# A two-layer delta-rule tower on one core: the second layer's products on four quarters of the array, values scaled by key lengths after the solve

## The chip, the cores and the metric

The kernel runs on one core of a Trainium2 chip. The metric is the device time of one execution in microseconds (us). One core has TensorE (PE in the profile, with its weight loads as PEld), VectorE (DVE), ScalarE (ACT), GpSimd (POOL) and SyncE (SP). Each takes its own instructions in order, and they wait for each other through semaphores.

## The reference, cut to what matters

The tower turns 16 images of 49 tokens (width 256) through two layers. Both have an attention that is a recurrence over tokens; the first layer has 4 heads, the second 16, each with 64 key and 64 value elements. The second layer's:

```python
q = q / (jnp.linalg.norm(q, axis=-1, keepdims=True) + EPS)
k = k / (jnp.linalg.norm(k, axis=-1, keepdims=True) + EPS)
alpha = jax.nn.sigmoid(h @ alpha_w + alpha_b).reshape(bsz, seq, H, DK)
beta = jax.nn.sigmoid(h @ beta_w + beta_b)
def step(s, inp):
    qt, kt, vt, at, bt = inp
    s = s * at[..., None]
    u = jnp.einsum('bhd,bhdv->bhv', kt, s)
    s = s + bt[..., None, None] * (kt[..., None] * (vt - u)[..., None, :])
    out = jnp.einsum('bhdv,bhd->bhv', s, qt)
    return (s, out)
...
y = y * jax.lax.rsqrt(jnp.mean(y * y, axis=-1, keepdims=True) + EPS) * head_norm_w
y = x + y @ out_w * gate
```

The first layer's has no decay `alpha`. Only the 16x49 outputs of the whole tower are returned, not the state.

## The kernel before, in words

The recurrence is not stepped through. For each image and head the kernel builds a 49x49 matrix A of key-key products and PT of key-query products, inverts a triangular system, and applies the result. An image pair lies on the 128 partitions: the even image's tokens on partitions 0 to 48, the odd one's on 64 to 112. All arithmetic on TensorE is f32; there each product of two f32 operands stands in the trace as two weight loads and two matmuls, a transpose as one of each.

The stages in order of time, with the time of the profile: patches and projections (0 to 65), the first layer's pairs, solve and applied products (65 to 122), layernorms and routing, the expert stage (181 to 280), the second layer's "level" stage (322 to 470: `small`, L1517, 32 products of 64x49 each in 56 calls on the four quarters of the array, with projections L1477 between), its solve (470 to 508), its applied products (510 to 575), the output projection (575 to 601), and two feed-forward parts.

Class `Delta` holds solve and application for both layers; the first uses its subclass `WideDelta`. For each layer:

- `dve_lengths` makes inverse key lengths (`inv_k`), `beta_k`, `beta_kk`. `pe_cols` and `pe_rows` turn beta and the rows of A into the layout of the solve (systems on partitions). In the second layer `pe_rows` is 48 transposes of 128x128, in 12 groups of 4 (L420); DVE multiplies each group by beta into `NS` (L459).
- `dve_solve`: 24 steps of two DVE instructions each (L473 and L479; in the first layer L809 and L815), each on what the last wrote.
- `pe_out` and `act_out` turn the solved rows back, on PE and ACT, during the solve; the second layer's value projections (L1528) fill PE there. `act_mask` scales A by a column (L519).
- `pe_apply`: for head h four products of 49x49 by 49x64, each for 8 image pairs and both partition halves, 16 matmuls: `d1` = U W (L570), `z` = A d1 (L580), `delta` = U W again after W was corrected (L591), `out` = PT delta (L602). Iteration i does d1 of head i, z of i-1, delta of i-3, out of i-5, so there are nh+5 iterations. Both inputs and output of a matmul lie on one partition half, so consecutive matmuls alternate between two diagonal quarters of the array. Each kind of product has two PSUM banks, used in turn by even and odd heads.
- Between them: ACT copies d1 (L655); DVE multiplies z by `inv_k` (L702) and POOL subtracts that from W (L394); ACT and DVE copy delta and out in turn; then squares, sums, root, reciprocal and a scaling by DVE (L731) make the normalised y, which PE turns (L554) and projects (L612).

What sets the order is this hand-written order of each engine's stream and the waits in it; nothing is scheduled by a program.

## Time and profile before

| | us |
|---|---|
| runs of before | 713.9, 717.19, 720.05 |
| their median | 717.19 |
| the profiled execution | 716.03 |
| its span, first to last instruction | 714.2 |
| PE busy in the span | 631.0 (88%) |
| granted TensorE clock, mean | 0.945 of full speed |

The profile is of one execution. In it 1.8 us lie outside the span. The page gives busy time by engine; the timeline gives instructions in order of time, and in square brackets the idle time of the engine before one and what ended it. "issue" there means that the engine waited for no semaphore that the profile shows. The DMA queue called "instruction" carries the engines' own programs from memory.

### The profile page before, as it was taken

The numbers are of one execution on the slowest core, as the hardware profiler recorded it, in microseconds if no ns is written. First come the engines' busy times: TensorE is split into PE (matmuls) and PEld (weight loads), VectorE is DVE, ScalarE is ACT, GpSimd is POOL, SyncE is SP. The second block draws the span as 40 slices with busy tenths as digits, with TensorE's granted clock in tenths as the row PEclk, the third lists the DMA queues.
The fourth block names the chain that finished last, engine by engine and source line by source line (L and its number), as shares of the span: only waits on it lengthen the run. The fifth ranks groups of instructions, "written<-read, shape, count | busy, mean of one in ns | idle before, by whom it ended". The sixth has DMA issues, their size and how long they took to land.

```text
span 714.2 us, 20162 instructions
## 1 busy us (share of the span) xinstructions
PE 631.0 (88%) x9124; PEld 463.7 (65%) x9124; DVE 329.0 (46%) x519; ACT 268.6 (38%) x538; POOL 144.4 (20%) x129
## 2 busy tenths in 40 slices
PE   8985497973899996699999997999899999999997
PEld 5654495673799995465655556665699966555563
DVE  0395735730011110356777779569536753411311
ACT  0354233211233232244666664548634443111223
POOL 9101030012000001712544446400133200000000
PEclk9997579996999999699999999799999999999999
DMA  9200000018989871100000201000000070000001
GB/s 315 110 0 2 4 3 2 1 36 313 409 316 335 324 268 33 49 15 31 26 27 26 84 4 62 3 3 0 2 5 4 5 295 1 1 0 0 1 1 45
DMA packets 20229, 56.38 MB, mean 79 GB/s; under 512 B 4272, under 2 KB 13104, under 8 KB 15792
## 3 DMA queue, kind: packets, MB, share of 16 engines
q1 hardware_dynamic: 19376, 53.00, 20.2%
q0 software_dynamic: 768, 2.10, 0.9%
q8 instruction: 72, 1.18, 0.7%
q14 instruction: 13, 0.11, 0.0%
HBM read 49.57 MB, written 5.52 MB: 77 GB/s over the span
## 4 chain that ended last, share of the span: by engine, by line
PE 73%; DVE 14%; issue 4%; ACT 3%; DMA 2%; POOL 2%; SPq 1%; DVEq 0%; ACTq 0%; POOLq 0%
PE PS L1477 8%; PE PS L1439 6%; PE PS L1517 6%; PE PS L1428 6%; PE PS L1614 6%; PE PS L612 4%; PE PS L1644 3%; PE PS L1621 3%; PE PS L570 3%; PE PS L591 3%; PE PS L580 3%; PE PS L602 3%; PE PS L1320 2%; PE PS L1334 2%; DVE arena L1773 2%
## 5 line engine op out<-in xcount | busy, mean ns | idle before, releaser
L1517 PEld LDWEIGHTS PS<-arena 64*49 64x49 f32 x3584 | 50.6, 124 | 37.2 <-issue 21.9
L1477 PE MATMUL PS<-Y,arena 128*128 128x392 f32 x192 | 73.3, 511 | 0.0
L1517 PE MATMUL PS<-arena 64*49 64x48 f32 (+2 forms) x3584 | 57.0, 214 | 11.1 <-DVE arena L1773 6.6
L1428 PE MATMUL PS<-arena 128*128 128x128 f32 x448 | 54.1, 280 | 4.8 <-DMA arena<-in_moe_b 4.2
L1768 DVE COPY_PREDICATED arena<-msk,PS 128x768 f32<-128x768 int32 x24 | 44.9, 1873 | 28.5 <-PE PS L1517 28.5
L1428 PEld LDWEIGHTS PS<-arena 128*128 128x128 f32 x448 | 53.5, 196 | 6.4 <-DMA arena<-in_moe_b 4.8
L1192 ACT ACTIVATE arena<-PS,arena 128x128 f32<-128x128 f32 x112 | 31.8, 369 | 65.2 <-PE PS L1428 65.2
L1130 POOL TENSOR_TENSOR arena<-arena 128x384 f32<-128x384 f32 (+1 forms) x32 | 36.1, 1128 | 78.5 <-PE PS L1517 73.9
L1439 PE MATMUL PS<-arena 128*128 128x256 f32 x224 | 50.5, 379 | 0.0
L394 POOL TENSOR_TENSOR arena<-arena,work 128x512 f32<-128x512 f32 x20 | 25.4, 1270 | 114.0 <-DVE work L702 114.0
L1477 PEld LDWEIGHTS PS<-Y,arena 128*128 128x128 f32 x192 | 33.2, 188 | 19.2
L1439 PEld LDWEIGHTS PS<-arena 128*128 128x128 f32 x224 | 41.5, 190 | 5.1
L1614 PE MATMUL PS<-work,arena 128*128 128x392 f32 x128 | 43.4, 491 | 0.8 <-issue 0.8
L1717 DVE COPY arena<-PS 128x256 f32<-128x256 f32 x14 | 5.9, 425 | 65.8 <-PE PS L1418 65.8
L1614 PEld LDWEIGHTS PS<-work,arena 128*128 128x128 f32 x128 | 24.0, 188 | 18.9 <-issue 1.1
L219 PE MATMUL PS<-fill 128*128 128x256 bf16 x236 | 31.5, 286 | 2.1 <-DVE fill L1667 2.1
L1103 POOL DMA_INDIRECT arena<-answers,place x8 | 7.6, 951 | 118.0 <-DMA answers<-arena 115.9
L1843 DVE TENSOR_TENSOR arena<-arena,PS 128x392 f32<-128x392 f32 x16 | 9.0, 563 | 47.2 <-ACT arena L1294 47.2
L702 DVE TENSOR_TENSOR work<-PS,inv_k 128x512 f32<-128x512 f32 x20 | 13.8, 690 | 34.6 <-PE PS L580 34.6
L219 PEld LDWEIGHTS PS<-fill 128*128 128x128 bf16 x236 | 23.6, 103 | 9.2 <-DVE fill L1667 2.1
L1528 PE MATMUL PS<-work,Y 128*128 128x512 f32 x64 | 29.0, 595 | 0.0
L612 PE MATMUL PS<-arena 128*128 128x392 f32 x80 | 27.7, 493 | 1.3 <-issue 1.3
(230 smaller groups left out, 1141.0 us busy)
## 6 DMA issues: line engine op xcount, KB each, us to landing
arena<-in_moe_w SPq DMA_DIRECT2D x28, 1024.0 KB, 6.3
arena<-in_qka_w SPq DMA_DIRECT2D x8, 384.0 KB, 3.1
arena<-in_patches SPq DMA_DIRECT2D x6, 392.0 KB, 6.6
arena<-in_ff_w SPq DMA_DIRECT2D x1, 2048.0 KB, 8.3
arena<-in_ffn_w SPq DMA_DIRECT2D x2, 1024.0 KB, 12.7
by_expert<-arena SPq DMA_DIRECT2D x1, 1792.0 KB, 12.7
arena<-in_moe_b SPq DMA_DIRECT2D x14, 128.0 KB, 7.4
arena<-by_expert SPq DMA_DIRECT2D x14, 128.0 KB, 6.9
```

Source lines behind the costliest of these rows:

```text
L219: nc.tensor.matmul(PS[:, i, 0:2 * P], fill[:, 0:P], fill, start=True, stop=True)
L394: nc.gpsimd.tensor_tensor(w, w, self.ZT[h % 2], ALU.subtract).then_inc(self.s["w_kept"], 1)
L612: m = nc.tensor.matmul(bank(4 + u), self.OW[:, f, (u // 2) * P:(u // 2 + 1) * P], half(self.OT[:, f], u % 2), start=(f == 0), stop=(f == n ...
L1130: nc.gpsimd.tensor_tensor(older, older, end, ALU.mult).then_inc(lv_keys, 1)
L1192: nc.scalar.activation(G[:, j % 2, f], PS[:, 4 + 2 * (j % 2) + f // 4, (f % 4) * P:(f % 4 + 1) * P], ACT.Gelu, bias=MB1[j % NW][:, f:f + 1 ...
L1428: m = nc.tensor.matmul(PS[:, 4 + 2 * (j % 2) + f // 4, (f % 4) * P:(f % 4 + 1) * P], MW1[j % NW][:, k, f * P:(f + 1) * P], XT[:, j % 2, k] ...
L1439: m = nc.tensor.matmul(PS[:, 2 + j % 2, 0:D], G[:, j % 2, f], MW2[j % NW][:, f], start=(f == 0), stop=(f == FT - 1))
L1477: m = nc.tensor.matmul(bank(i % 3), GW[g % 2][:, k, u // 2], half(Y[:, k], u % 2), start=(k == 0), stop=(k == KT - 1))
L1517: m = nc.tensor.matmul(o, K[r, b, :], v, start=True, stop=True)
L1528: m = nc.tensor.matmul(PS[:, value_bank(u), :], Y[:, k, 2 * b:2 * b + 2].rearrange("p b t -> p (b t)"), VW[:, k, n * 512:(n + 1) * 512], s ...
L1614: m = nc.tensor.matmul(bank(4 + 2 * n + cc), FW13[:, k, cc, f * P:(f + 1) * P], half(SQ[:, k], n), start=(k == 0), stop=(k == KT - 1))
L1768: nc.vector.copy_predicated(dst, mk, src).then_inc(lv_kept, 1)
```

## The change

It does the following:

1. The values are scaled once, before the products: POOL multiplies each head's W by the key lengths kept in `root`. In the second layer POOL waits for the last solve step, in the first only for the lengths. W is then corrected by a single DVE subtraction out of PSUM; POOL's subtraction, `inv_k`'s masking and `beta_k` go. Correspondingly the first 25 token columns of A are cleared and only the rest masked (`act_mask` and `act_clear`).
2. In the second layer (`PARTS` 2) a product's input half and output half are chosen apart: for a pair of images the four matmuls go to quarters (0,0), (0,1), (1,0), (1,1). The result of odd images lands on the other partition half, so A and PT of every second image pair are built swapped already in `small`. A product now uses both banks of its kind, so head h waits until head h-1 is copied away (`ahead` 1, before 2). The number of matmuls is unchanged.
3. The second layer's `pe_rows` is no longer 48 full transposes but 192 ordinary matmuls of 64 partitions by 49 columns on the four quarters, in 6 groups of 32; DVE takes 6 products twice as large.
4. The second layer's final scaling of y moves from DVE to POOL; squares, sums and roots stand one iteration later in both layers.
5. The first layer (`PARTS` 1) keeps its two banks in turn and its order of matmuls.

```diff
-            NGI = (T - 1) // 4
+            NGI = (T - 1) // 8
-            def pool_apply(self, pool):
-
+            def pool_apply(self, pool, values_kept):
+
+                pool.wait_ge(*values_kept)
+                if self.PARTS == 2:
+                    self.wait(pool, "step", 2 * (BL - 1))
+                else:
+                    self.wait(pool, "lengths", self.n_lengths)
                 for h in range(self.nh):
-                    self.wait(pool, "z_kept", h + 1)
                     w = self.W[:, :, h * DH:(h + 1) * DH]
-                    nc.gpsimd.tensor_tensor(w, w, self.ZT[h % 2], ALU.subtract).then_inc(self.s["w_kept"], 1)
+                    key = root[:, self.S + h * BP:self.S + (h + 1) * BP].unsqueeze(2).broadcast_to([P, BP, DH])
+                    nc.gpsimd.tensor_tensor(w, w, key, ALU.mult).then_inc(self.s["w_scaled"], 1)
+                if self.PARTS == 2:
+                    for j in range(self.nh // 2):
+                        self.scale(pool, nc.gpsimd, j)
...
-                for r in range(4):
-                    m = nc.tensor.transpose(PS[0:self.S, g % 4, r * P:(r + 1) * P],
-                                            self.Am[:, :, 1 + 4 * g + r], c("ident"))
+                for r in range(8):
+                    for place_ in range(2):
+                        for odd in range(2):
+                            p = slice(TP * place_, TP * place_ + TP)
+                            m = nc.tensor.matmul(
+                                PS[TP * odd:TP * odd + TP, 2 * (g % 2) + (place_ + odd) % 2, r * TP:r * TP + T],
+                                self.Am[p, odd::2, 1 + 8 * g + r], c("ident")[p, TP * place_:TP * place_ + T],
+                                start=True, stop=True)
...
+            def product(self, i, h, operands):
+
+                for pair in range(0, BP, 2):
+                    for r, o in ((0, 0), (0, 1), (1, 0), (1, 1)):
+                        b = (r + o) % 2
+                        if self.PARTS == 1:
+                            r, b, o = o, r, o
+                        lhsT, rhs = operands(self.part(r), pair + b)
+                        m = nc.tensor.matmul(self.place(i, h, self.part(o), pair + b), lhsT, rhs, start=True, stop=True)
+                return m
...
+                        self.wait(pe, "w_scaled", h + 1)
+                        if h >= self.ahead:
+                            self.wait(pe, "d1_kept", h + 1 - self.ahead)
...
-                        nc.vector.tensor_tensor(
-                            self.ZT[h % 2], PS[:, 2 + h % 2, :].rearrange("p (b v) -> p b v", b=BP),
-                            inv_k[:, h * BP:(h + 1) * BP].unsqueeze(2).broadcast_to([P, BP, DH]),
-                            ALU.mult).then_inc(self.s["z_kept"], 1)
+                        nc.vector.tensor_tensor(self.head(h), self.head(h), self.result(1, h), ALU.subtract) \
+                            .then_inc(self.s["w_kept"], 1)
...
-                            o = PS[TP * (b % 2):TP * (b % 2) + T, pb + hd]
+                            c_ = (b + pair) % 2
+                            o = PS[TP * c_:TP * c_ + T, pb + hd]
```

The order of PE's instructions at the start of the second layer's solve, before; L1517 are the last level products, L420 the rows of A turned by transposes, L1528 value projections:

```order
L1517 MATMUL PS<-arena 49x64 x32
L411 MATMUL PS<-con,beta_kk 128x128
L412 MATMUL PS<-con,beta_k 128x128
L1528 MATMUL PS<-work,Y 128x512 x2
L1517 MATMUL PS<-arena 49x64 x32
L420 MATMUL PS<-con,arena 128x128 x48
L1528 MATMUL PS<-work,Y 128x512 x6
L502 MATMUL PS<-con,arena 128x128 x8
```

The same place after the change; L1566 is L1517 of before, L438 the rows of A, L1577 the value projections:

```order
L1566 MATMUL PS<-arena 49x64 x32
L426 MATMUL PS<-con,beta_kk 64x128 x2
L1577 MATMUL PS<-work,Y 128x512 x2
L1566 MATMUL PS<-arena 49x64 x32
L438 MATMUL PS<-con,arena 64x49 x192
L1577 MATMUL PS<-work,Y 128x512 x6
L521 MATMUL PS<-con,arena 128x128 x8
```

Nothing moved there, but 48 instructions became 192, and these are ordinary f32 products, which count twice in the trace.

POOL's last instructions, before; L394 is the subtraction from W:

```order
L387 MEMSET arena 128x3400
L387 MEMSET arena 128x2x25
L1130 TENSOR_TENSOR arena<-arena 128x16x6x4
L1133 TENSOR_TENSOR arena<-arena 128x16x6
L1130 TENSOR_TENSOR arena<-arena 128x16x2x8
L1133 TENSOR_TENSOR arena<-arena 128x16x3
L1121 TENSOR_TENSOR arena<-arena 128x16
L394 TENSOR_TENSOR arena<-arena,work 128x8x64 x16
```

And after the change; L398 scales W by the key lengths, L407 is the final scaling of y that DVE had:

```order
L386 MEMSET arena 128x3400
L386 MEMSET arena 128x2x25
L1175 TENSOR_TENSOR arena<-arena 128x16x6x4
L1178 TENSOR_TENSOR arena<-arena 128x16x6
L1175 TENSOR_TENSOR arena<-arena 128x16x2x8
L1178 TENSOR_TENSOR arena<-arena 128x16x3
L1166 TENSOR_TENSOR arena<-arena 128x16
L398 TENSOR_TENSOR arena<-arena,root 128x8x64 x16
L407 TENSOR_TENSOR arena<-arena,y_var 128x8x128 x8
```

The sixteen instructions on W keep their place in POOL's stream but no longer wait for each head's z, and eight on y come behind them.

## Rows read from the trace of the kernel before

**Rows 1.** The page, parts 1 (busy us, share, instructions) and 3 (packets, MB, share).

```profile
PE 631.0 (88%) x9124; PEld 463.7 (65%) x9124; DVE 329.0 (46%) x519; ACT 268.6 (38%) x538; POOL 144.4 (20%) x129
q8 instruction: 72, 1.18, 0.7%
```

**Rows 2.** Busy time of each engine in three stretches.

```profile
core 0: us, PE busy (x) PEld busy (x) DVE busy (x) ACT busy (x) POOL busy (x), PEclk, DMA share, GB/s
76.60:92.40 15.80, 6.91 (x196) 6.00 (x196) 13.09 (x48) 4.46 (x15) 0.00 (x0) 0.50 0.01 3
470.30:477.40 7.10, 6.94 (x58) 6.27 (x52) 4.50 (x14) 2.07 (x2) 0.00 (x0) 1.00 0.02 3
509.90:574.80 64.90, 62.03 (x2064) 60.06 (x2065) 36.62 (x55) 30.03 (x53) 20.28 (x16) 1.00 0.04 7
```

**Rows 3.** Timeline of weight loads, second layer's products: start, us, engine, line, idle before.

```profile
537.88 0.17 PEld L580 LDWEIGHTS PS<-arena 49*49 49x49 f32 x3 [0.27 <-issue]
...
540.64 0.88 PEld L580 LDWEIGHTS PS<-arena 49*49 49x49 f32 x28
541.81 0.17 PEld L580 LDWEIGHTS PS<-arena 49*49 49x49 f32 x4 [0.29 <-issue]
...
556.34 1.01 PEld L580 LDWEIGHTS PS<-arena 49*49 49x49 f32 x32
557.24 1.01 PEld L591 LDWEIGHTS PS<-arena 49*49 49x49 f32 x32
```

**Rows 4.** DMA of 532 to 544 us: GB/s in 40 slices, the instruction queue.

```profile
GB/s 0 0 0 0 0 0 0 0 0 0 55 0 0 0 0 0 0 0 0 0 0 0 0 55 0 0 0 0 0 0 0 0 0 0 0 0 55 0 0 0
...
q8 instruction: 3, 0.05, 2.0%
```

**Rows 5.** DMA of 554 to 564 us, the same two rows.

```profile
GB/s 0 0 66 0 0 0 0 0 0 0 0 0 0 0 0 0 66 0 0 0 0 0 0 0 0 0 0 0 0 0 0 66 0 0 0 0 0 0 0 0
...
q8 instruction: 3, 0.05, 1.9%
```

**Rows 6.** DMA of 466 to 482 us, GB/s in 40 slices of 0.4 us.

```profile
GB/s 0 0 0 0 0 0 0 0 0 0 41 0 0 0 20 0 0 0 0 0 0 0 0 0 0 0 0 0 0 0 0 0 0 20 0 0 0 41 0 0
```

**Rows 7.** Timeline of PE in the level stage, products on four quarters.

```profile
348.51 1.12 PE L1517 MATMUL PS<-arena 64*49 64x64 f32 x64
349.56 1.58 PE L1477 MATMUL PS<-Y,arena 128*128 128x392 f32 x4
...
354.36 1.68 PE L1517 MATMUL PS<-arena 64*49 64x49 f32 x128
355.97 1.25 PE L1477 MATMUL PS<-Y,arena 128*128 128x392 f32 x3
```

**Rows 8.** Timeline at the start of the second layer's solve.

```profile
472.63 4.06 PE L420 MATMUL PS<-con,arena 128*128 128x128 f32 x32 [0.16 <-ACT arena L1237]
473.41 3.68 DVE L459 TENSOR_TENSOR arena<-PS,sys_cols 128x192 f32<-128x192 f32 x8 [0.54 <-PE PS L420]
477.36 0.35 DVE L473 TENSOR_TENSOR work<-arena 128x96 f32<-128x96 f32 x1
```

**Rows 9.** Timeline where DVE and POOL both read two operands from SBUF.

```profile
339.26 1.77 DVE L1773 TENSOR_TENSOR arena<-arena 128x1568 f32<-128x1568 f32 x1
339.57 2.01 POOL L1130 TENSOR_TENSOR arena<-arena 128x256 f32<-128x256 f32 x1 [2.77 <-PE PS L1517]
340.96 1.67 DVE L1796 TENSOR_TENSOR arena<-arena 128x384 f32<-128x384 f32 x2
```

**Rows 10.** Instructions of POOL's line L394: duration min, median, max in ns.

```profile
L394 POOL TENSOR_TENSOR arena<-arena,work x20: 1263/1270/1276, 98.1 to 564.7; 128x512 f32<-128x512 f32 x20
```

**Rows 11.** Timeline of the first layer: lengths, start of the solve, first products.

```profile
73.03 0.19 DVE L436 TENSOR_TENSOR beta_kk<-beta_k,inv_k 128x32 f32<-128x32 f32 x1
...
76.58 0.20 DVE L809 TENSOR_TENSOR work<-arena 128x24 f32<-128x24 f32 x1 [0.52 <-DVE arena L801]
...
92.47 3.65 PE L570 MATMUL PS<-arena 49*49 49x64 f32 x64 [0.69 <-issue]
```

More of the change, by code:

```diff
@@ L378, in wait @@
                 eng.wait_ge(self.s[name], self.before.get(name, 0) + value)
-            NGI = (T - 1) // 4
+            NGI = (T - 1) // 8
             NGO = len(GROUPS)
-            ZT = [work[:, 1024 + 512 * i:1536 + 512 * i].rearrange("p (b v) -> p b v", b=BP) for i in range(2)]
             def pool_clear(self, pool):
@@ L542, in kept, with place, result, ahead @@
                     self.wait(eng, f"{what}_{('even', 'odd')[h % 2]}", h // 2 + 1)
+            def product(self, i, h, operands):
[7 more added lines that the diff above has]
+                return m
+            def place(self, i, h, part, b):
+                if self.PARTS == 2:
+                    return PS[part, 2 * i + b % 2, (b // 2) * DH:(b // 2 + 1) * DH]
+                return PS[part, 2 * i + h % 2, b * DH:(b + 1) * DH]
+            def result(self, i, h):
+                if self.PARTS == 2:
+                    return PS[:, 2 * i:2 * i + 2, 0:BP // 2 * DH].rearrange("p a (m v) -> p a m v", v=DH)
+                return self.pairs(PS[:, 2 * i + h % 2, :].rearrange("p (b v) -> p b v", b=BP))
+            @property
+            def ahead(self):
+                return 3 - self.PARTS
+            def pairs(self, x):
+                return x.rearrange("p (m a) v -> p a m v", a=2)
+            def head(self, h):
+                return self.pairs(self.W[:, :, h * DH:(h + 1) * DH])
             def pe_apply(self, pe, between=None):
@@ L586, in pe_apply @@
                         self.wait(pe, "w_kept", h + 1)
-                        self.kept(pe, "delta", h - 2)
-                        for b in range(BP):
-                            for cc in range(2):
-                                r = self.part(cc)
-                                m = nc.tensor.matmul(PS[r, 4 + h % 2, b * DH:(b + 1) * DH],
-                                                     self.U[r, h, b, :], self.W[r, b, h * DH:(h + 1) * DH],
-                                                     start=True, stop=True)
-                        m.then_inc(self.s["delta_mm"], 1)
+                        self.kept(pe, "delta", h - self.ahead)
+                        self.product(2, h, lambda r, b: (self.U[r, h, b, :], self.W[r, b, h * DH:(h + 1) * DH])) \
+                            .then_inc(self.s["delta_mm"], 1)
                     h = i - 5
@@ L597, in pe_apply @@
                         self.kept(pe, "delta", h)
-                        self.kept(pe, "out", h - 2)
-                        for b in range(BP):
-                            for cc in range(2):
-                                r = self.part(cc)
-                                m = nc.tensor.matmul(PS[r, 6 + h % 2, b * DH:(b + 1) * DH],
-                                                     self.PT[r, h, b, :], self.D[r, h, b, :], start=True, stop=True)
-                        m.then_inc(self.s["out_mm"], 1)
+                        self.kept(pe, "out", h - self.ahead)
+                        self.product(3, h, lambda r, b: (self.PT[r, h, b, :], self.D[r, h, b, :])) \
+                            .then_inc(self.s["out_mm"], 1)
                     if 0 <= i - self.nh - 1 < self.EARLY:
@@ L640, in keep_out @@
                 self.wait(eng, "out_mm", h + 1)
-                op(self.W[:, :, h * DH:(h + 1) * DH],
-                   PS[:, 6 + h % 2, :].rearrange("p (b v) -> p b v", b=BP)).then_inc(self.s[f"out_{('even', 'odd')[h % 2]}"], 1)
+                op(self.head(h), self.result(3, h)).then_inc(self.s[f"out_{('even', 'odd')[h % 2]}"], 1)
             def keep_delta(self, eng, op, h):
                 self.wait(eng, "delta_mm", h + 1)
-                op(self.D[:, h], PS[:, 4 + h % 2, :].rearrange("p (b v) -> p b v", b=BP)) \
+                op(self.pairs(self.D[:, h]), self.result(2, h)) \
                     .then_inc(self.s[f"delta_{('even', 'odd')[h % 2]}"], 1)
             def act_apply(self, act, between=None):
-                for i in range(self.nh + 8):
+                for i in range(self.nh + 9):
                     if between is not None:
@@ L694, in dve_apply @@
             def dve_apply(self, dve):
-                for i in range(1, self.nh + 9):
+                for i in range(1, self.nh + 10):
                     h = i - 1
```

131 lines of the change are left out of this document (67 added, 64 removed).

## The prediction

> **What bounds the kernel now.** The page comes first: PE is busy 88% of the span, so the path runs mostly through PE [rows 1]. The windows by stage come next, for the stages that the change touches. In the second layer's applied products PE shows 62 of 64.9 us busy, DVE 37, ACT 30, POOL 20 [rows 2]. Read alone, this says that PE's arithmetic is the bound and that twice the quarters should nearly halve the stage. In the first layer's solve DVE is busy 13.1 of 15.8 us [rows 2], a chain of dependent steps.
>
> The timeline of the weight loads says something else about the applied products. A product is 16 matmuls, so 32 loads and 32 matmuls in the trace, and undisturbed ones follow each other every 0.90 us (556.34 to 557.24). But at 537.88 and at 541.81 PE stops in the middle of a product for "issue", which is no semaphore, and goes on with the last 3 or 4 loads [rows 3]. From one restart to the next are 3.93 us where four products take 3.6. The loads between the restarts are 3 + 32 + 32 + 32 + 28 = 127 (three rows of 32 are left out), with as many matmuls and a few waits: 256 instructions.
>
> The page has 9124 loads and as many matmuls, with about 250 waits 18,500 instructions, and 72 transfers on the instruction queue, of 1.18 MB / 72 = 16.4 KB [rows 1]: again one per 256 instructions. The DMA view places them. In 532 to 544 us, slices of 0.3 us, they begin in slices 10, 23 and 36, that is at about 535.1, 539.0 and 542.9, 3.9 us apart; 2.0% of 16 engines over 12 us is 3.84 us, 1.28 us each [rows 4]. So the transfer begun at 535.1 ends at 536.4, PE restarts 1.45 us later at 537.88, and the next transfer begins 1.2 us after that. I read this as a loop: entering a block of 256 instructions asks for the next, whose transfer starts 1.2 us later, and it can be used 1.4 us after its end. One round is 2.6 us plus the transfer. At 554 to 564 us a transfer took 1.9% x 160 / 3 = 1.01 us, they begin 3.5 to 3.75 us apart [rows 5], the loop needs 3.6, four products need 3.6, and no stall stands there [rows 3]. The stage is therefore already at the edge of two limits, arithmetic (3.6 us per iteration) and the supply of instructions (3.6 to 3.9, on the average of the stage's transfers, 1.1 us, 3.7).
>
> The Trainium skill (Runtime: NRT & Kernel Launch, Instruction fetch mechanics) says that instructions are refilled in 16 KiB blocks of 256, which the trace agrees with, and that PE's store holds 2048 of them and crossing a block's edge is "mostly hidden". The stalls of 0.27 and 0.29 us [rows 3] speak against the second half. By the page the sum would be that of rival 1, by the row that of the forecast.
>
> **The change part by part.** *Applied products, second layer.* Their number stays 64, with 64 instructions each, 4096. Four-quarter products are in the trace: 64 loads of 49 columns with 64 columns streamed take 349.56 - 348.51 = 1.05 us, and 128 with 49 streamed take 1.61 us [rows 7]. A new product, 32 loads, is then 0.40 to 0.53 us of PE; I take 0.50, near the row with 64 columns, but its operand is contiguous. Arithmetic needs 4 x 0.50 = 2.0 us per iteration, DVE and ACT somewhat above 2, the instruction supply still 3.7. So the supply sets the pace. With the waits the stage is about 4190 instructions. Counted in blocks of 256 back from the restart at 541.81 and then forward through the changed stream, an edge stands some 175 instructions into the stage; the blocks up to there and one beyond are at hand, and PE enters the second about 1.9 us in, held by the chain d1, copy, d1. Fifteen more edges come at 3.7 us: 57.4 us. The last 170 instructions, the last copy of out and the two turns take 3.9 as they do now. That is 61.3 against 64.9: **-3.6 us** (transfers of 1.0 us: -5; of 1.2 us: -2). What has only one set of banks now (head h waits for the copy of h-1) costs nothing here: each product has 0.93 us on average while a copy takes 0.6 to 0.7. That cover goes if the supply is not the limit.
>
> POOL's scaling of W starts when the solve ends. One is 1.27 us like L394 [rows 10], about what `pe_out` and `act_out` need behind the last step anyway, and the next heads come every 1.25 us, faster than they are used. Sixteen take 20 us. The scalings of y have twice the elements, 2.5 us each, eight in a stage where two heads take 7.4 us, and the last must be ready only when the projection reaches it, seven periods of 3.5 us later. Both 0, as is the moved DVE work.
>
> *`pe_rows`, second layer.* Before: 48 transposes, 96 instructions, from 470.3 with the last 32 at 472.63 for 4.06 us, then the first solve step at 477.36 [rows 8]. Behind stands the whole solve, in which DVE never rests, so a delay here moves everything. New: 192 matmuls, 768 instructions, three blocks. Arithmetic alone would be 6 x 0.81 us (32 matmuls of 49 columns [rows 7]), a little less than now. The supply: by the same count an edge stands 114 instructions before the first one, so the next stand at 149, 405 and 661. A transfer begins in slice 10 of 0.4 us, at 470.4 [rows 6], and the block is usable at 470.4 + 1.1 + 1.4 = 472.9. The edges are then passed at 472.9, 476.6 and 480.3 (3.7 each), and the remaining 107 instructions take 0.7: 481.0. The last DVE multiply (twice 192 elements; 0.36 us for 192 at most, from L459 [rows 8]; 0.6 taken) and the diagonal: first step at 482.0, **+4.6 us**. Bounds 3.7 to 5.5, by transfers of 0.8 to 1.4 us. If no block is late it is -0.6.
>
> *First layer.* The lengths are done near 73.2 [rows 11], and POOL then runs four scalings of 1.25 us, to 78.3. The solve begins at 76.58, and each of its instructions reads two operands in SBUF. Such instructions exclude POOL's: at 339.57 a POOL multiply of 256 elements starts under a DVE one and shows 2.01 us, until 341.58, and the two DVE instructions issued at 340.96 show 1.67, so they end 1.05 us after 341.58 [rows 9]; nobody ran until the other had ended. So the first step waits for the third scaling (about 77.0), the second for the fourth (78.5): +1.9 us in a chain that PE waits for. Four small matmuls and a DVE step less give 0.2 back. **+1.7 us** (0, if DVE always wins, to 2.5). Its products keep order and pitch: 0. The Trainium skill (SBUF — State Buffer, Who interferes with whom) tells of the same lock and lets the first to issue keep it.
>
> *Level stage.* Where odd image pairs come in swapped order, a quarter is used again after 3 matmuls instead of 4. With 48 or 49 columns that is still enough; with 64, 3 x 33 = 99 ns lie under the 107 that one needs (128 cycles at 2.4 GHz, twice). Bounds 0 and 16 calls x 0.05 us = 0.8; **+0.3 us**.
>
> Sum: -3.6 + 4.6 + 1.7 + 0.3 = **+3.0 us**. The profiled execution took 716.0, 1.2 under the median. So 719.0 against it, 720.2 against the median; I forecast 720. Its own range is 715 to 725.
>
> **The rivals.** *1. Instructions are at hand, arithmetic bounds.* For it speak PE's busy share and that the stalls before are only 0.3 us; against it the equal distance of transfer, restart and transfer in rows 3 to 5. Then the stage is bounded by DVE, about 35 us of work with the scalings of y gone [rows 2], and PE 64 x 0.50 = 32, with some 7 us to fill and drain: 42, so -23. `pe_rows` gives -0.6, the other two +2.0: -21.6, about 695. Chance 0.12, with cases halfway (two blocks ahead).
>
> *2. The clock falls, the other side.* PE now works 2.0 us of each 3.7 in the stage. In the first layer's solve, with PE 6.9 of 15.8 us busy, the granted clock is 0.50 [rows 2], 1.2 of 2.4 GHz, and two products then take 3.65 us instead of 1.8 [rows 11]. At half clock a four-quarter product is 1.0 to 1.06 us and an iteration 4.0 to 4.25, above the supply's 3.7. It decides from 3.7 / 4 = 0.93 us per product, a clock under 0.57. Over 15 iterations up to +8 us: 728. Against it: the second layer's solve keeps its clock. Chance 0.08.
>
> *3. The supply bounds, but `pe_rows` is spared,* since a block more was ready there in the calm before. Then +3.0 - 4.6 = -1.6, 715.5. The first part of the stage before was short of nothing at 470 [rows 8], but 768 instructions are more than any two blocks. Chance 0.12.
>
> **How the numbers follow.** Forecast 0.68, rivals 0.12, 0.08 and 0.12. About 1% of this kernel, 7 us, can be told from no change. Forecast and rival 3 lie within it, but for the forecast's upper end (first layer 2.5, rows 5.5, products 0: +9) with 0.07. Faster by over 1%: 0.12; slower: 0.15; within: 0.73. The range 712 to 727 leaves out rival 1 and the far end of rival 2.
>
> **What the profile after would show.** Transfers on the instruction queue in the applied products still 3.5 to 3.9 us apart, PE idle for "issue" about 1.7 us per iteration, products of 0.5 us; 75 transfers in all; the first solve step of the second layer 4 to 5 us later behind the last level product, with PE stopped for "issue" twice or three times inside L438; the first layer's L809 and L815 with one or two instructions of over 1 us. I am wrong if transfers come 2.5 us apart, if the products' stage is under 50 us, or if the granted clock falls in it.

## The result, and the profile after

The changed kernel is slower: 730.9 us median of four runs (728.3 to 740.2) against 718.6 (713.9 to 720.1), a ratio of 1.0191 with a 95% interval of 1.0135 to 1.0247. The execution of 740.2, with a mean granted clock of 0.87 against 0.90 to 0.92 in the others, counts as a slow one and is left out of the ratio. In a later session it was 728.9 against 717.5, ratio 1.0158 (1.0111 to 1.0204). The forecast was 720, the range 712 to 727. The profiled execution took 728.33 us, its span is 726.0 (before 716.03 and 714.2), so the two traces differ by 11.8 us of span.

The page after, parts 1 and 3 (compare [rows 1]), and busy time by stage (compare [rows 2]; the first stretch is the first layer's solve, then `pe_rows`, then the second layer's products):

```profile
PE 621.7 (86%) x9454; PEld 451.9 (62%) x9454; DVE 320.0 (44%) x503; ACT 269.8 (37%) x540; POOL 154.6 (21%) x137
q8 instruction: 75, 1.23, 0.7%
```

```profile
core 0: us, PE busy (x) PEld busy (x) DVE busy (x) ACT busy (x) POOL busy (x), PEclk, DMA share, GB/s
76.50:93.60 17.10, 6.90 (x197) 6.03 (x197) 14.29 (x48) 4.47 (x15) 2.31 (x5) 0.50 0.01 3
476.60:489.90 13.30, 12.91 (x405) 12.31 (x394) 3.51 (x7) 2.06 (x2) 0.00 (x0) 0.87 0.02 6
522.60:586.60 64.00, 40.37 (x2064) 36.63 (x2065) 30.16 (x49) 30.08 (x52) 24.00 (x20) 0.92 0.02 4
```

In the products PE is busy 40.4 us instead of 62.0, and the stage is only 0.9 us shorter (64.0 for 64.9). `pe_rows` and what stands between it and the first solve step takes 13.3 us instead of 7.1. Timeline of the weight loads in the products (compare [rows 3]):

```profile
535.99 1.85 PEld L585 LDWEIGHTS PS<-arena 49*49 49x49 f32 x126 [1.44 <-issue]
539.94 5.34 PEld L585 LDWEIGHTS PS<-arena 49*49 49x49 f32 x252 [2.10 <-issue]
546.81 1.85 PEld L585 LDWEIGHTS PS<-arena 49*49 49x49 f32 x126 [1.53 <-issue]
550.81 1.85 PEld L585 LDWEIGHTS PS<-arena 49*49 49x49 f32 x126 [2.15 <-issue]
554.82 1.85 PEld L585 LDWEIGHTS PS<-arena 49*49 49x49 f32 x126 [2.17 <-issue]
558.32 1.80 PEld L585 LDWEIGHTS PS<-arena 49*49 49x49 f32 x124 [1.65 <-issue]
```

126 loads with their matmuls and waits are one block of 256 instructions. They are done in 1.85 us, and then PE stands for "issue" until the next block is there, 3.5 to 4.0 us after the last one. That is the pattern that the forecast described. Timeline of `pe_rows` and the first solve step after (compare [rows 8]):

```profile
476.63 2.45 PEld L438 LDWEIGHTS PS<-con,arena 64*64 64x64 f32 x75
479.60 9.35 PEld L438 LDWEIGHTS PS<-con,arena 64*64 64x64 f32 x309 [0.52 <-issue]
...
489.94 0.33 DVE L492 TENSOR_TENSOR work<-arena 128x96 f32<-128x96 f32 x1
```

Only the first of the three block edges stops PE. After it 309 loads run without a pause and take 9.35 us, 30 ns each. In the first layer (timelines of POOL and DVE; compare [rows 10, 11]):

```profile
73.33 4.05 POOL L398 TENSOR_TENSOR arena<-arena,root 128x512 f32<-128x512 f32 x4 [9.78 <-DVE beta_kk L455]
...
75.64 0.78 DVE L846 COPY arena<-sys_cols 128x25 f32<-128x25 f32 x1
76.53 0.89 DVE L854 TENSOR_TENSOR work<-arena 128x24 f32<-128x24 f32 x1
77.45 0.35 DVE L860 TENSOR_TENSOR arena<-arena,work 128x24 f32<-128x24 f32 x1
77.83 0.33 DVE L854 TENSOR_TENSOR work<-arena 128x46 f32<-128x46 f32 x1
...
77.34 1.47 POOL L1136 TENSOR_TENSOR arena<-con,par 128x128 f32<-128x128 f32 x4
```

A copy that took 0.18 us and a first step's first instruction that took 0.20 take 0.78 and 0.89 under POOL's scalings. The copy costs nothing, since the solve begins as long behind the rows as before (5.0 us). A scaling takes 1.04 us, not 1.27, so they end at 77.4 and hold up one instruction of the solve for long. Behind them run four short multiplications of POOL (L1136), which before stood beside the first layer's products. Under them four instructions of the solve take 0.33 to 0.35 us instead of 0.21 to 0.23. Of the 1.2 us by which the first product comes late, 0.7 are that first instruction and 0.5 these four.

The shift between the two traces, read at the start of the same instructions, gives the sum by stage (us, rounded; `pe_rows` runs from its first load to the first solve step):

| stretch | forecast | measured |
|---|---|---|
| rows to first product, first layer | +1.7 | +1.2 |
| first product to the experts' end, same code but for order | 0 | +3.3 (1.0, 0.6, 2.4, then -0.7) |
| gather and norm to the first level product | 0 | +1.2 |
| level stage but its last call | +0.3 | -0.3 |
| last level call, same work | 0 | +1.0 |
| `pe_rows` | +4.6 | +6.3 |
| second solve | 0 | 0.0 |
| applied products | -3.6 | -0.8 |
| sum, before rounding | +3.0 | +11.8 |

### The profile page after: what moved, and what is told of

Read it like the earlier page. It is cut to its first block and busy times, and to the rows that moved or that the text cites. A ratio compares the mean times of both kernels' runs of the same rounds, so it can differ in the third digit from the quotient of the medians.

```text
span 726.0 us, 20823 instructions
## 1 busy us (share of the span) xinstructions
PE 621.7 (86%) x9454; PEld 451.9 (62%) x9454; DVE 320.0 (44%) x503; ACT 269.8 (37%) x540; POOL 154.6 (21%) x137
## 5 line engine op out<-in xcount | busy, mean ns | idle before, releaser
L585 PE MATMUL PS<-arena 49*49 49x64 f32 x2560 | 55.4, 230 | 23.7 <-issue 20.8
L1566 PEld LDWEIGHTS PS<-arena 64*49 64x49 f32 x3584 | 50.9, 125 | 36.8 <-issue 21.4
L585 PEld LDWEIGHTS PS<-arena 49*49 49x49 f32 x2560 | 51.7, 131 | 27.9 <-issue 25.2
L1566 PE MATMUL PS<-arena 64*49 64x48 f32 (+2 forms) x3584 | 57.2, 215 | 10.7 <-DVE arena L1822 6.7
L1766 DVE COPY arena<-PS 128x256 f32<-128x256 f32 x14 | 5.9, 425 | 65.5 <-PE PS L1466 65.5
L398 POOL TENSOR_TENSOR arena<-arena,root 128x512 f32<-128x512 f32 x20 | 20.1, 1044 | 56.8 <-DVE arena L498 47.0
L1577 PE MATMUL PS<-work,Y 128*128 128x512 f32 x64 | 29.2, 599 | 0.0
```

Of the source, the lines that this page charges most:

```text
L585: m = nc.tensor.matmul(self.place(i, h, self.part(o), pair + b), lhsT, rhs, start=True, stop=True)
L1566: m = nc.tensor.matmul(o, K[r, b, :], v, start=True, stop=True)
L1577: m = nc.tensor.matmul(PS[:, value_bank(u), :], Y[:, k, 2 * b:2 * b + 2].rearrange("p b t -> p (b t)"), VW[:, k, n * 512:(n + 1) * 512], s ...
```

## The experiments

**1. Is the supply of instructions the pace of the products?** Two kernels from the changed one.

```
# half_products                                   # more_instr, ahead of each matmul of layer 2
-for pair in range(0, BP, 2):                     +nc.tensor.matmul(self.place(...)[:, 0:1], lhsT, rhs[:, 0:1],
+for pair in range(0, BP, 2 * self.PARTS):        +                 start=True, stop=True)
```

> The changed kernel, with every second pair of matmuls of the second layer's applied products left out (32 instructions a product instead of 64; 2048 in the stage instead of 4096). The output is not the reference's. Copies on ACT and DVE, scalings on POOL and the waits are all unchanged. Changed kernel: 64.0 us from the first L585 load to the first load of the projection, restarts 3.7 us apart. Supply theory: 7 to 8 block edges instead of 15; the supply alone would need 28 us, so the chain through ACT and DVE sets the pace and the stage takes 40 to 46 us, with blocks taken less often than every 3.7 us and few or no stops at their edges. Rival (the single set of banks, that is the chain product, copy, next product, sets the pace and the stops are only its shadow): nothing of that chain but 0.25 us per product has gone, and the stage stays at 58 us or more.

> The changed kernel, with a matmul of one column ahead of each matmul of the second layer's applied products, into the same place and overwritten by it: 128 instructions a product instead of 64, 8192 in the stage, the same result. PE stands idle 1.4 to 2.0 us of each 3.7 in the changed kernel, and the added loads and matmuls need at 12 to 16 ns a pair about 1.5 to 2 us of it. Supply theory: an iteration is two blocks and takes 2 x 3.7 = 7.4 us, the stage 15 more edges x 3.7 = +55 us, the whole kernel about 780 to 788. Rival (arithmetic, or the chain of copies, bounds and the supply does not): the additions fit into PE's idle time, the stage takes 64 to 75 us.

Measured, from the first load of the products to the first of the projection: 40.6 us with half the instructions, 120.5 us with twice as many (+56.5 for +55 forecast), and the whole kernels took 710.5 and 782.9 us, one execution each. Both numbers are those of the supply theory. But the granted clock fell in both. The stage in half_products, in more_instr and in after_fill (the changed kernel with other work ahead of it, experiment 3):

```profile
526.50:567.10 40.60, 34.79 (x1042) 31.13 (x1041) 28.92 (x49) 29.21 (x52) 23.99 (x20) 0.58 0.01 3
519.20:639.70 120.50, 107.49 (x4112) 100.16 (x4112) 30.77 (x50) 31.13 (x53) 24.36 (x20) 0.54 0.02 4
514.20:579.00 64.80, 52.98 (x2065) 49.27 (x2065) 30.29 (x49) 30.59 (x52) 24.36 (x20) 0.68 0.02 4
```

In more_instr PE is busy 107.5 of 120.5 us at a mean clock of 0.54, so PE's own work is nearly as long as the supply's: this run alone doesn't tell them apart. What speaks for the supply there are stops of 0.4 to 1.1 us for "issue" at most block edges. In half_products transfers come 4.5 us apart on average, so the supply is no longer the pace there; whether the 40.6 us are the chain of copies or PE at the lower clock is not separated. The cleaner evidence is the third row. Over nine profiles of the stage in quarters with 4096 instructions PE is busy between 40.4 and 53.0 us, at mean clocks from 0.92 down to 0.68, and the stage takes 62.8 to 67.2 us without following it: 64.0 at 40.4, 64.8 at 53.0. PE's arithmetic is not the pace. DMA of 540 to 556 us in more_instr, slices of 0.4 us:

```profile
GB/s 0 0 0 41 0 0 0 0 0 0 0 0 41 0 0 0 0 0 0 0 0 41 0 0 0 0 0 0 0 0 41 0 0 0 0 0 0 0 41 0
q8 instruction: 5, 0.08, 2.1%
```

Transfers begin every 3.5 us here, and every 3.7 on average of the stage. Over the fifteen profiles of the products with 4096 instructions, on the diagonal or in quarters, the mean distance is 3.7 to 3.9 us and the mean transfer 1.03 to 1.12.

**2. Why do `pe_rows`' loads take 30 ns?** rows_probe changes the stationary operand from group to group, rows_swap the count of matmuls.

```
# rows_probe: groups 3, 4          lhsT = self.W[p, 0, TP * (2 * r + odd):TP * (2 * r + odd) + TP]
# rows_probe: groups 5, 6          lhsT = self.Am[p, odd:odd + 2 * T - 1:2, 1 + 8 * g + r]
# rows_swap: 96 matmuls over all 128 rows; for odd systems x is the identity with halves exchanged
+x = bass.AP(x.tensor, x.offset + TP, [x.ap[0], [-TP, 2], [1, TP]])
+m = nc.tensor.matmul(o, self.Am[:, odd::2, 1 + 8 * g + r], x, start=True, stop=True)
```

> The changed kernel, with other operands in the second layer's pe_rows: groups 1 and 2 as they are (64 stationary columns, read 196 bytes x 2 apart), groups 3 and 4 with 64 stationary columns that lie side by side (taken from W), groups 5 and 6 with 49 columns at the old distance. The output is not the reference's, since four of six groups turn other numbers. In the changed kernel L438 issues its 384 loads in 12.0 us, about 30 ns each, with one stop of 0.5 us only, where the prediction had 12.6 ns each and stops at two more block edges. Theory A (the distance between the columns makes a load long, so that quarters don't overlap): groups 3 and 4 take 0.8 to 1.0 us each without the stops, groups 5 and 6 about 1.5 (49/64 of 2.0), and PE stops for issue once or twice in or behind groups 3 and 4, since 256 instructions then need less than the supply's 3.7 us. Theory B (the width or the form of the tile, 64 columns for 49): groups 3 and 4 stay at 2.0 us, groups 5 and 6 fall to 0.8. Theory C (the supply of instructions paces it smoothly): all six groups stay near 1.9 us.

The timeline of L443's loads in rows_probe: the four stretches begin behind the stops at block edges.

```profile
471.73 2.45 PEld L443 LDWEIGHTS PS<-con,arena 64*64 64x64 f32 x75
474.70 2.83 PEld L443 LDWEIGHTS PS<-con,arena 64*64 64x64 f32 x128 [0.52 <-issue]
478.17 2.62 PEld L443 LDWEIGHTS PS<-con,arena 64*64 64x64 f32 x128 [0.63 <-issue]
481.89 1.36 PEld L443 LDWEIGHTS PS<-con,arena 64*49 64x49 f32 x53 [1.10 <-issue]
```

(The distance is 784 bytes, two systems of 98 elements, not 2 x 196 as my expectation had it.) By start-to-start distances without the stops, a load took 29.5 ns in groups 1 and 2, 15 ns in groups 3 and 4 (side by side) and 22.7 in groups 5 and 6 (49 columns at a distance). Theory A holds, theories B and C fall: where loads are short, the three stops that the forecast expected are there (0.5, 0.6, 1.1 us); where they are long, PE is the slower one and no further stop is seen behind the first.

> The changed kernel, with pe_rows by 96 matmuls over all 128 rows instead of 192 over 64: one matmul turns 64 systems of one token, and for odd systems the identity is read with its halves exchanged. So 96 x 64 = 6144 stationary columns are loaded at a distance (twice, since f32 is loaded twice), against 12288 in the changed kernel and 6144 in 48 transposes before. Theory A (columns at a distance take 0.46 ns each per load, whatever the tile: rows_probe showed 29.5 ns for 64 of them, 22.7 for 49, and 15 ns for 64 side by side): L438 takes 5.7 us with a stop of about 0.6 us, 12.1 before it, and the kernel is 5.5 to 6.5 us faster than the changed one, 724 to 726 against its median of 730.9. Rival (the count of instructions bounds, 384 of them at 3.7 us per 256): the same 5.6 us, but with stops at the block edges; then the loads show under 25 ns. If pe_rows were not on the path, nothing changes.

Both answers fell, and so did the forecast of 724 to 726 us. L441 in rows_swap:

```profile
474.68 11.53 PEld L441 LDWEIGHTS PS<-con,arena 128*64 128x64 f32 x192
```

Half the loads, 59 ns each, the same 11.3 us start to start, and 729.7 us (ratio 1.0184, 1.0144 to 1.0225). So the price is not by column. For an operand at a distance it is by element: 64 x 64 elements take 29.5 ns, 128 x 64 take 59, and 128 x 128, the transposes before (392 bytes apart), 118 ns. What doubled is the number of loads per element: a matmul in f32 shows two loads, a transpose one (48 transposes are 48 loads in L420). 48 x 118 = 5.7 us before, 384 x 29.5 = 11.3 after, 192 x 59 = 11.3 here.

> both_swap with the even systems' rows turned by a transpose instead of a matmul with the identity (the odd ones stay matmuls with the exchanged identity). In rows_swap 192 loads of 64 columns took 11.3 us, 59 ns each, so the cost is not by column as I had thought but by element: 64 x 64 elements at a distance take 29.5 ns, 128 x 64 59 ns, 128 x 128 118 ns (48 transposes before, each with one load). A matmul in f32 loads its operand twice, a transpose once. Theory: the even half falls from 96 loads to 48, the rows take 144 x 59 ns = 8.5 us and the stop of 0.5, 2.8 us less than in both_swap. Rival (a transpose loads twice as well, or costs more per load): 11.3 us as in both_swap.

Measured: 744.0 us (1.0378). The transposes do show one load each and the matmuls two, but the 48 rows take 33 us, with the matmuls in L444 and the transposes in L446 (loads by line: count, busy us, mean ns, idle before):

```profile
L444 PEld LDWEIGHTS PS<-con,arena 128*64 128x64 f32 x96 | 14.9, 204 | 5.8
L446 PEld LDWEIGHTS PS<-con,arena 128*64 128x64 f32 x48 | 6.6, 137 | 5.8
```

That is 0.69 us per row instead of 0.24, far more than the 0.18 of its three loads: a transpose and a matmul in turn cost something of their own that this run doesn't split up. So the count of loads is seen, the gain from it could not be seen here. diagonal_l0 (experiment 4) shows it: it goes back to 48 transposes, in the 6 groups of the changed kernel but with the systems in the old order.

**3. What did the first layer cost?** l0_two takes half of POOL's scalings away from the solve; before_late puts the delay alone into the kernel before.

```
# l0_two, in pool_apply                       # before_late, ahead of the first step, five times
+if h == 2 and self.PARTS == 1:               +self.wait(dve, "unit", 1 + i)
+    self.wait(pool, "step", 2 * (BL - 1))    +nc.vector.tensor_copy(work[:, 0:P], c("ident")).then_inc(...)
```

> The changed kernel, with two of the first layer's four scalings of W on POOL moved behind the last step of its solve (the first two still run beside the lengths, from 73.3 to 75.4 us, the solve's first step comes at 76.5). Theory A (POOL's operations held up the solve): L854 and L860 show 0.2 us from the first step on, as in the kernel before, and the first product comes 1.1 us earlier behind the rows, 20.9 us instead of 22.0. Theory B for the clock (PE stays at 1.2 GHz longer only because of where the delayed solve puts the products): the first product to the first turn takes 21.4 instead of 22.4, the turn and projection 7.8 instead of 8.4, the routing 6.9 instead of 9.3; the kernel is 5 us faster, 726. Rival for the clock (it is the products' other order, or chance): only the 1.1 us come back, 729.8.

> The changed kernel once more, beside the same runs of before, for its median in the same session: 728 to 732 and a ratio near 1.018. l0_two measured 721.2 against it, 9.7 us less, of which 5 are explained (1.1 of solve, 4 at the lower clock). If the rest is chance of the runs, this median comes out lower, 726 to 728; if the scalings on POOL cost more than I know, it stays at 731.

base_after is the 728.9 us already given. l0_two: 721.2 us (1.0078, 1.0039 to 1.0116), more than the 5 us that I had expected. The medians differ by 7.7 us, but they come from two sessions; by the two ratios (1.0158 and 1.0078) it is 5.7. The first steps show 0.20 us again, and the first product comes 20.4 us behind the rows instead of 22.0. That is 1.6 us. From there to the end of the routing the profile is 4.1 us shorter, at the higher clock; what it gains behind that I leave to the scatter of single executions. Windows from the first product to the first turn, and of the routing that follows (PEclk is the column before the last two), in this order: before, the changed kernel, l0_two.

```profile
92.40:114.00 21.60, 16.65 (x513) 16.51 (x513) 9.60 (x15) 7.21 (x12) 6.51 (x8) 0.90 0.01 3
143.10:149.90 6.80, 6.80 (x52) 6.69 (x52) 1.59 (x7) 2.64 (x8) 0.00 (x0) 0.84 0.00 0
...
93.60:116.10 22.50, 17.64 (x512) 17.39 (x512) 9.54 (x15) 7.21 (x12) 0.00 (x0) 0.80 0.01 3
145.80:155.10 9.30, 9.21 (x52) 9.08 (x52) 1.59 (x7) 3.06 (x8) 0.00 (x0) 0.63 0.00 0
```

```profile
91.30:112.90 21.60, 16.64 (x513) 16.43 (x513) 9.60 (x15) 7.21 (x12) 2.46 (x6) 0.90 0.01 3
142.00:148.80 6.80, 6.79 (x52) 6.66 (x52) 1.59 (x7) 2.63 (x8) 0.00 (x0) 0.84 0.00 0
```

The granted clock has two levels, 0.50 and 1.00 (1.2 and 2.4 GHz), and the mean tells how long each stood. The same 52 matmuls take 6.8 us at a mean of 0.84 and 9.3 at 0.63; in the products 1.0 us is lost in the same way. I call 21.3 to 21.8 us with 6.8 or 6.9 behind it the short form, 22.2 to 22.6 with 9.3 the long one. All six profiles of kernels that carry the four early scalings (and no filling, below) have the long form. A second profile of the kernel before has the short one:

> The kernel before, once more, for a second profile of the stretches that the change doesn't touch. Between the two profiles the routing to the experts begins 1.6 us later than the first layer's end explains, the levels 1.2 us and the solve 1.3 us more: 4 us in stretches with the same code. Theory A (the time at half clock in these stretches varies from execution to execution, and has nothing to do with the change): this execution shows differences of 1 us or more to the first profile of before in the same stretches. Theory B (the later end of the first layer moves work so that PE's clock falls or recovers later): this execution repeats the first profile within 0.3 us in each stretch.

It took 21.3 and 6.9 us. In the stretches up to the levels it repeats the first profile within 0.3 us (theory B), but its second solve, at lower clock in between, took 2.7 us longer with the same code (theory A). Both are true in their place.

> The kernel before, with five dependent copies of 128 columns on DVE (about 0.23 us each) between the rows and the first step of the first layer's solve, so that this solve ends some 1.2 us later; nothing else is changed, the result is the same. Theory (a first product that comes 22.0 us behind the rows instead of 20.4 to 20.9 meets a lower clock for longer: in four executions of the changed kernel's kind TensorE rose to 2.4 GHz 5.6 to 6.3 us after the first product, in four with the early one 3.6 to 4.2 us after it, and the routing that follows took 9.3 instead of 6.8 us): the delay of 1.2 us costs 4 to 5.5 us, about 722 to 724, first product to first turn 22.3 to 22.6 us instead of 21.3 to 21.6, turn and projection 8.3 instead of 7.8, routing 9.3 instead of 6.9. Rival (the longer time at the lower clock comes from the changed kernel's order of products, or is chance): 1.2 us, 719.5.

Measured 720.3 (1.0042, 1.0009 to 1.0075), 2.9 over the 717.5 beside it. The profiled execution, one of its fastest, shows the delay (22.0 us) but the short form behind it, 21.8 and 6.8 us. Its twelve timings fall into two groups, three from 714.3 to 716.4 and nine from 719.1 to 722.7. The kernel before has such times too without the delay, but fewer (5 of 21 from 719.3 to 721.4 beside it). So the delay seems to make the long form frequent, not certain; that the nine are the long form is inferred from their times, not seen in a trace. both_swap (below) has the long form in its profile without the delay. When the granted clock changes is thus not bound to the kernel's steps: it rises 4.1 us after the first product in the kernel before and 4.5 in before_late, 6.3 in the changed kernel, and 4.2 in l0_two but 6.1 in both_swap, which have the same first layer. The Trainium skill (TensorE: Matmul & The Clock Gate, Part 1) says that the hardware's watch on activity doesn't start with the kernel; that the same code meets the rise at different places agrees with it.

The last question was whether the clock is all of it. Matmuls whose result nobody reads fill PE's waits of the first layer:

```
+spin(12, 6)                                       # ahead of pe_sums, and behind pe_cols
+spin((24, 14, 14, 14, 14, 6, 4, 0)[g], 6)         # ahead of each group of the first layer's pe_out
```

> The kernel before, with 114 matmuls of 256 bf16 columns whose result nobody reads, in PE's waits of the first layer: 12 ahead of pe_sums, 12 behind pe_cols, 24, 14, 14, 14, 14, 6 and 4 ahead of the groups of pe_out. At 2.4 GHz one takes 0.11 us, so they fit in the waits for DVE's solve; at 1.2 GHz they would not. Theory (activity on PE keeps the clock up, and the lower clock is what stretches this part): the granted clock stays at 1.00 from 63 us to the end of the first layer, the first product to the first turn takes 19.5 to 20 us instead of 21.3 to 21.6, the routing 6.9 or less; the kernel is 2 to 5 us faster, 713 to 716. Rival (the clock falls in spite of them): the added matmuls take twice as long, the groups of pe_out come late, 720 to 723.

> The same matmuls in the changed kernel. Theory: the clock stays up here too, first product to first turn as in before_fill, and up to the first turn the kernel differs from before_fill by 1.2 us alone, those of POOL's scalings; the median falls by 4 to 6 us, to 723 to 726, and what is left against before_fill is 8 to 10 us, of which 6 are pe_rows. Rival (something else of the change stretches the first layer): a difference to before_fill of 2 us or more up to the first turn.

> diagonal_l0 (0.9996 of the kernel before) with the same matmuls. Theory: clock up in the first layer, 2 to 5 us faster than diagonal_l0: 710 to 713, ratio 0.990 to 0.995, faster than both kernels. Rival: the clock is no better, 715 or more.

First product to first turn, in before_fill and after_fill:

```profile
92.60:112.30 19.70, 14.73 (x513) 14.50 (x513) 9.62 (x15) 7.21 (x12) 6.51 (x8) 0.96 0.01 3
```

```profile
92.30:111.90 19.60, 14.69 (x512) 14.47 (x512) 9.56 (x15) 7.21 (x12) 0.00 (x0) 0.99 0.01 3
```

The clock stays at 1.00 (2.4 GHz) until 110 us in both, and the two kernels are equal there: nothing but the clock stretched the changed one in its products. after_fill takes 722.2 us (ratio to before 1.0092, 1.0058 to 1.0127; the changed kernel's was 1.0158), a gain of 4.7 us by the ratios and 6.8 by the medians of two sessions. before_fill gains nothing (718.6, 1.0013), where 2 to 5 us had been expected. Its trace shows where the 1.9 us that it wins in the products go. First, its first product comes 22.0 us behind the rows instead of 20.9, because PE stops for "issue" inside `pe_cols` (before_fill, weight loads), as at a block edge that the added instructions have moved there; in after_fill a stop of 0.97 us falls between added matmuls and costs nothing. Second, behind 110 us its clock falls for longer, and the routing has the long form:

```profile
74.92 0.10 PEld L767 LDWEIGHTS PS<-con,beta_kk 64*32 64x32 f32 x1 [1.28 <-issue]
...
142.50:151.40 8.90, 8.88 (x52) 8.88 (x53) 1.60 (x7) 3.07 (x8) 0.00 (x0) 0.64 0.00 0
```

after_fill has 6.8 us there. So the filling holds the clock where it stands, and doesn't settle the form of what follows. diagonal_fill, with 8.9 us in its routing too, took 714.7 (0.9975, 0.9940 to 1.0011), not the expected 710 to 713: not faster than the kernel before by what can be told.

**4. Are the quarters worth anything?**

> Both edits of rows_swap and l0_two in the changed kernel. If they are independent, as both theories say: 6 us for pe_rows and 1.1 to 5 us for the first layer, 720 to 724, that is 0 to 0.7% above the kernel before. What is left of the change is then the applied products on four quarters, which take 64 to 66 us for 64.9 and 65.5 before.

> As both_swap, but without the quarters: the second layer's products, its level products and its rows in the layout of the kernel before (two quarters on the diagonal, two sets of banks in turn, 48 transposes), while the scaling by key lengths on POOL and the fused subtraction on DVE stay as changed. Supply theory: the products keep their pace, 4096 instructions at 3.7 us per 256, arithmetic 3.6; the stage takes 64 to 66 us as with quarters, and the kernel ends within 2 us of both_swap. Rival (quarters pay): the stage takes 2 to 4 us more than in both_swap.

both_swap: 722.6 (1.0088, 1.0048 to 1.0127). diagonal_l0: 714.7 (0.9996, 0.9963 to 1.0028), 7.9 less, more than either theory said. By their traces: 5.4 us are `pe_rows` (5.98 for 11.35 us, as rows_swap's 96 matmuls saved nothing), 3.6 the products, with 62.9 us on the diagonal and 66.5 in quarters. The two profiled executions differ by 14.4 us, more than the medians: both_swap's is one of its longest. All profiles of quarters took 62.8 to 67.2 us (mean of nine 65.1), of the diagonal 62.2 to 65.5 (mean of six 63.6). The quarters are worth nothing here. Products on the diagonal and in quarters (windows of diagonal_l0 and both_swap):

```profile
508.70:571.60 62.90, 61.13 (x2064) 59.78 (x2064) 30.72 (x49) 30.02 (x52) 23.84 (x20) 1.00 0.02 4
```

```profile
519.60:586.00 66.40, 47.49 (x2064) 43.37 (x2064) 30.15 (x49) 29.96 (x52) 23.92 (x20) 0.79 0.02 4
```

**5. Why 64 us once and 67 another time?** edge_swap moves the places of the block edges.

```
+if g == 2:                                  # in the second layer's pe_out
+    for _ in range(32):
+        nc.tensor.matmul(PS[0:32, 2 * (g % 2), 0:1], c("ident")[0:TP, 0:32], c("ident")[0:TP, 0:1], ...)
```

> both_swap with 32 matmuls of one column (128 instructions) ahead of pe_out's third group, in the middle of the second solve, where PE's work is hidden behind DVE. both_swap and rows_swap have 384 instructions less than the changed kernel ahead of the applied products, so that a block edge stands there 49 instructions into the stage instead of 177, and the stage took 66.5 and 67.2 us, against 64.0 and 62.8 in the changed kernel and l0_two. Theory (the place of the edges decides how much of the last block's time is added to the stage's tail): with the edges back at 177 the stage takes 62.5 to 64.5 us. Rival (it is the clock or chance): 66 to 67 us.

The stage took 64.3 us instead of 66.5 (721.9, ratio 1.0073). That fits the theory, but the changed kernel, base_after, l0_two and rows_probe all have their edges at 177 and took 64.0, 65.6, 62.8 and 66.4. Single stages scatter by as much as the effect, so this is not shown.

## Why the prediction was wrong

The traces differ by 11.8 us where the sum said 3.0. Three terms failed, in order of size: what a later first product does to the granted clock behind it was put at nothing and came with 3.3 us; the applied products were put at -3.6 and gave -0.8; `pe_rows` was put at +4.6 and cost 6.3, by another mechanism. Another 2.2 us fell in stretches for which no cause is shown. The first layer's delay and the level stage came out 1.1 us better than forecast.

*Supply of instructions in the products:* right, by the equal distance of the transfers and by a stage that doesn't follow PE's busy time (experiment 1). A product takes 0.47 us of PE (126 loads in 1.85 us, 32 a product) for 0.50, and restarts come 3.7 us apart (528.96 to 577.26 us, 13 intervals). *The stage's sum, -3.6,* was too good by 2.8: the first late restart came 6.4 us in instead of 5.6 (its transfer took 1.32 us), the fourteenth at 54.7 instead of 53.7, and from there to the projection it took 9.3 us instead of 7.6, with a mean clock of 0.74 from 575 to 587 us. None of the nine profiles in quarters reached the forecast 61.3 us; against the six on the diagonal there is no gain at all. Rivals 1 and 3 did not come.

***`pe_rows`, +4.6,* is the step whose mechanism failed.** "Arithmetic alone would be 6 x 0.81 us" took the price of a matmul from the level products [rows 7], whose stationary columns lie side by side. The operation's own row was at hand: 32 loads of L420 in 4.06 us [rows 8]. Those columns lie at a distance, 118 to 127 ns a load, and a matmul loads twice what a transpose loads once. 2 x 5.7 = 11.3 us plus one stop of 0.5 would have given +6. The supply, which I let set the pace, is the faster of the two there. That +4.6 came within 1.7 us of the measurement is luck: two stops that never came stood in for the price of the loads. The Trainium skill (SBUF — State Buffer, Door 1: The DMA port swizzle) says that an access which crosses to a new 16-byte line pays a penalty; the trace agrees, 29.5 against 15 ns for the same 64 x 64. It should have been weighed against this change.

*First layer, +1.7:* the mechanism was right (0.89 us for the first step under POOL's scaling), the size 1.2: a scaling takes 1.04 us and so holds up one instruction, and 0.5 us came from POOL's L1136, which the forecast had not seen moving beside the solve. **What the sum lacked, the largest error,** is what hangs on this delay: +3.3 us by the end of the experts, at a lower clock. Taking the scalings away brought it back (l0_two), and the delay alone brought it in part (before_late, 2.9 us for 1.2). I had priced the clock only in the second layer's products, though [rows 11] showed the first products at half clock. There it did fall (0.92 in this trace, 0.68 to 0.81 in the eight others), which was named as a sign of being wrong, and cost little, as rival 2 said it would above a clock of 0.57.

*Level stage, +0.3:* -0.3 measured, nothing: the price of reusing a quarter after three matmuls was not there. A call with 64 columns takes 1.04 us from start to start after the change (354.10 to 355.14) and 1.05 before. The other +2.2 us, in the gather and in the last level call, are the clock again by their windows (0.81 for 0.83, 0.79 for 0.84). I don't put them down to the change: the five executions that share the changed kernel's code up to there (after, base_after, rows_probe, half_products, more_instr) took 31.4 to 33.4 us for the gather (33.1 in the profile after, 31.9 before) and differ by 1.5 us in the level stage.

## What to carry to other kernels

Take the price of an operation from its own row, with its layout, before that of another with the same shape: here a stationary operand read at a distance took time by its elements, in quarters or not, and an f32 matmul in place of a transpose doubled the loads. Before work is made cheaper on an engine, count its instructions: here 256 of them came every 3.7 to 3.9 us on average, so a stage with short matmuls is bound by their number. And a small delay ahead of a stretch that begins at the lower clock can cost more than twice its length (2.9 us for 1.2 in before_late).

## What the runs showed of the hardware

- A load of a stationary f32 operand whose columns lie 784 bytes apart takes 29.5 ns for 64 x 64 elements and 59 for 128 x 64, against 15 for 64 x 64 side by side. It does not follow the clock: with a granted clock of 0.50 (1.2 GHz, 483 to 485 us in the changed kernel) it still takes 29.7 ns.
- A transpose and a matmul in turn: 0.69 us for one of each (even_turned), where two such matmuls take 0.24 (rows_swap).
- Instructions for PE: about 3.7 us per 256 in a stage that wants them faster, with transfers of 1.03 to 1.12 us and, in four cases of five, 2.4 to 3.0 us from a transfer's end to the start of the next (fifteen profiles).
- POOL multiplications of 128x128, in a row, stretch DVE's two-operand instructions beside them from 0.21 to 0.23 us to 0.33 to 0.35 (changed kernel, 77.3 to 78.8 us).
